# A post-norm decoder layer: the context projected in tiles of 125 tokens instead of batch by batch

## The reference

```python
x = layernorm(x + self_attention(x))            # 16 heads of 16, rotary
x = layernorm(x + cross_attention(x, ctx))      # 16 heads of 64
x = layernorm(x + mixture_of_experts(x))        # 14 experts, top 1

# cross attention
Q = einsum('bsd,hdk->bhsk', queries, WQ) + bQ
K = einsum('btd,hdk->bhtk', keys, WK) + bK
V = einsum('btd,hdv->bhtv', values, WV) + bV    # keys and values are both the context
scores = Q @ K / 8
allowed = (key <= query) & (key < length[b])
concat = softmax(where(allowed, scores, -1e6)) @ V
out = concat @ WO + bO
```

## Time and profile before

| | |
|---|---|
| runs shown | 529.42, 529.50, 530.25 us, median 529.5 |
| profiled execution | 529.48 us |
| its span, first to last instruction | 527.7 us |
| mean granted TensorE clock | 0.96 |
| busy PE / DVE / ACT / POOL | 89% / 67% / 58% / 40% |

### The profile page before, as it was taken

One profiled execution on the slowest core, in us unless ns is written; L12 is line 12 of the kernel. 1 busy time (PEld: TensorE's weight loads), 2 busy tenths in 40 slices (PEclk: granted clock), 3 DMA queues, 4 the chain that ended last, 5 costly groups with the idle time before them and its releaser, 6 DMA issues. The chain is left out here.

```text
span 527.7 us, 12522 instructions
## 1 busy us (share of the span) xinstructions
PE 471.4 (89%) x4430; PEld 402.1 (76%) x4430; DVE 353.8 (67%) x971; ACT 304.2 (58%) x1400; POOL 211.1 (40%) x293
## 2 busy tenths in 40 slices
PE   1688899999998999999999999999999763999991
PEld 0566688878797888778887988788798662999981
DVE  1699686867869875887669658963745544255553
ACT  2266575888575674677576667783846612333330
POOL 1457543454246544443343433731413302144443
PEclk9899799999999999999999999999999985899997
DMA  5971444402600406304314104100405523999100
GB/s 167 203 163 43 166 169 166 162 2 101 220 8 22 162 17 232 114 0 160 135 34 144 45 1 153 47 1 2 161 1 181 186 115 100 368 371 372 44 25 17
DMA packets 38200, 63.03 MB, mean 119 GB/s; under 512 B 10435, under 2 KB 31412, under 8 KB 37419
## 3 DMA queue, kind: packets, MB, share of 16 engines
q1 hardware_dynamic: 34742, 33.03, 20.5%
q10 hardware_dynamic: 926, 25.83, 13.9%
q0 software_dynamic: 2464, 3.31, 2.0%
HBM read 58.85 MB, written 29.77 MB: 168 GB/s over the span
## 5 line engine op out<-in xcount | busy, mean ns | idle before, releaser
L972 ACT ACTIVATE probs<-bank,neg_max 100x100 f32<-100x100 f32 x512 | 169.8, 369 | 28.9 <-DVE neg_max L1096 18.0
L886 POOL TENSOR_TENSOR probs<-probs,row_inv 100x400 f32<-100x400 f32 x128 | 109.6, 877 | 110.4 <-DVE row_inv L1101 110.2
L972 ACT ACTIVATION_READ_ACCUMULATOR probs<-bank,neg_max 100x1 f32 x512 | 117.8, 230 | 0.0
L1096 DVE TENSOR_REDUCE neg_max<-bank 100x4 f32<-100x400 f32 x128 | 67.9, 565 | 9.9 <-PE bank L1367 4.8
L1401 PE MATMUL bank<-ident,probs 100*100 100x100 f32 x512 | 67.8, 255 | 5.7 <-DVE probsT L1108 4.1
L1401 PEld LDWEIGHTS bank<-ident,probs 100*100 100x100 f32 x512 | 50.4, 130 | 18.6 <-issue 7.5
L981 ACT COPY probsT<-bank 100x400 f32<-100x400 f32 x60 | 29.8, 497 | 47.2 <-PE bank L1401 41.5
L1245 PE MATMUL bank<-cT_h,W_K 128*128 128x200 f32 x256 | 50.6, 284 | 0.7 <-DVE kX L1024 0.6
L1318 PE MATMUL bank<-yT,W_Q 128*128 128x250 f32 (+1 forms) x224 | 50.3, 367 | 0.0
L1108 DVE COPY probsT<-bank 100x400 f32<-100x400 f32 x68 | 38.7, 569 | 16.3 <-PE bank L1401 14.4
L1245 PEld LDWEIGHTS bank<-cT_h,W_K 128*128 128x128 f32 x256 | 41.6, 193 | 2.5 <-DVE kX L1024 1.3
(11 more groups left out here) (153 smaller groups left out, 972.6 us busy)
## 6 DMA issues: line engine op xcount, KB each, us to landing
expert_rows<-c_empty ACTq DMA_DIRECT2D x13, 1935.0 KB, 8.9
w<-in_L_ffn_w_dram SPq DMA_DIRECT2D x36, 512.0 KB, 6.8
cs<-in_ctx_dram SPq DMA_DIRECT2D x16, 100.0 KB
...
```

Source lines behind the costliest of these rows:

```text
L886: probs_ready.mark(pool.tensor_tensor(v, v, r, ALU.mult), step)
L972: i = act.activation(probs[:, k % SLOTS, w], sc_bank[p % 2 * 2 + u][0:T, w], ACT.Exp, bias=neg_max[:, k % SLOTS, h:h + 1], accum_out=row_s ...
L1096: max_ready.mark(dve.tensor_reduce(neg_max[:, k % SLOTS, :], src, AX_X, ALU.max, negate=True), step)
```

## The change

- The context is loaded, turned and split in the 13 tiles of 125 tokens. A tile's rows come from two batches, so `c_load.n` is now up to two DMAs into one slot of `cs`, each with its own look at the length. `cT` holds 250 tokens.
- Keys are projected for two tiles, 250 columns at a time (7 groups instead of 8; the last has 100 columns). `kX` is a ring of 500 tokens.
- Values are projected per tile: `V.t.c` (13 tiles instead of 16 batches) goes to a staging buffer `v_tile` with one slot for each half, through a plain copy by DVE or ACT (`V_out_v`, `V_out_a`). A new step `move.b.c.t`, a DMA on SP's queue, copies the rows of tile t that belong to batch b from `v_tile` to `vX`. There are 50 of them, of 25 to 100 rows of 2 KB. `pv.x.b.c` waits for their landing, `V_out` of tile t+1 waits for the landing of tile t's moves, and a move waits for `V_out` and for `pv.x.(b-2).c`.
- The bias of the values goes through WO once: `vb_hi` (ACT) and `vb_lo` (DVE) spread and split it, `vb.0` (PE, 24 matmuls of 256 columns) multiplies it by WO, and `vb_out` (DVE) adds it to `o_bias`. `v_bias` is loaded as 128 x 8 by eight small DMAs that stand at the end of SP's first DMAs; the broadcast of 100 x 1024 is gone.
- `Y2S` goes from 6 to 4, `cs` slots are 125 rows, the buffer `fix` shares space with `oX`. `check` of batch 2 moves ahead of the list.
- `STEPS` is a new list throughout.

```diff
-Y2S = 6
+Y2S = 4
...
-check.2 check.3 xT.0 check.4 xT_hi.0 bias.s.0 xT_lo.0 check.5 w_hi.0 xT.1 check.6 w_hi.1 w_lo_v.0 bias.s.1 xT_hi.1
...
+check.3 xT.0 check.4 xT_hi.0 bias.s.0 xT_lo.0 check.5 w_hi.0 xT.1 check.6 w_hi.1 w_lo_v.0 bias.s.1 xT_hi.1 w_lo_v.1
...
+check.13 check.14 qkT.0 qk_out.1 qkT_out_a.0 check.15 xT.3 rot.1 xT_hi.3 keys_p.0 cT.1 w_hi.5 c_load.3 xT_lo.3
+bias.s.3 scores.s.0.0 rot_sum.1 cT_hi.1 w_lo_p.5 cT_lo.1 cT.2 max.s.0.0.0 qkT.1 c_load.4 max.s.0.0.1 exp.s.0.0.0
...
+def shared_rows(b, t):
+    first, last = max(T * b, TT * t), min(T * (b + 1), TT * t + size(t))
+    return slice(first - T * b, last - T * b), slice(first - TT * t, last - TT * t)
...
-            v_bias = ab("v_bias", [T, DC])
+            v_bias = ab("v_bias", [P, PAIRS])
...
-            cT = [ab(f"cT_{p}", [P, CTS, KC, KB * T], F32R) for p in "hl"]
+            cT = [ab(f"cT_{p}", [P, KC, QT], F32R) for p in "hl"]
...
-            kX = ab("kX", [P, 2, PAIRS, KB * T])
+            kX = ab("kX", [P, PAIRS, RT])
             vX = ab("vX", [T, 2, DC])
+            v_tile = ab("v_tile", [TT, 2, DC // 2])
...
+            def values_there(b, c, t=None):
+                k = 2 * (b % 2) + c
+                parts = sum(len(tiles_of(n)) for n in range(b % 2, b, 2)) + (len(tiles_of(b)) if t is None else t - tiles_of(b)[0] + 1)
+                return v_moved[k], 16 * parts
...
+                elif kind == "V":
+                    if step[1]:
+                        for b in batches_of(step[1] - 1):
+                            wait(*values_there(b, n, step[1] - 1))
...
                 def load_c(n):
-                    wait(ctx_fixed, n + 1)
                     if n >= 2:
                         wait(*projected.at(("cT", n - 2)))
-                    length = sp.value_load(len_row[0:1, n:n + 1])
...
+                    for b in batches_of(n):
+                        wait(ctx_fixed, b + 1)
+                        of_batch, of_tile = shared_rows(b, n)
+                        length = sp.value_load(len_row[0:1, b:b + 1])
...
+                            sp.dma_start(cs[of_tile, n % 2, :], ctx[b, of_batch, :]).then_inc(c_in[n % 2], 16)
+
+                def move(b, c, t):
+                    wait(*taken(("V", t, c)))
+                    if b >= 2:
+                        wait(*pv_done.at(("pv", "x", b - 2, c)))
+                    of_batch, of_tile = shared_rows(b, t)
+                    sp.dma_start(vX[of_batch, b % 2, c * (DC // 2):(c + 1) * (DC // 2)], v_tile[of_tile, c, :]).then_inc(v_moved[2 * (b % 2) + c], 16)
...
-                    (v_bias[:, :], bV.rearrange("(o h) k -> o (h k)", o=1).broadcast_to([T, DC])),
...
+                bias_by_head = bV.rearrange("(c w i u) d -> c i u d w", c=2, w=2, i=2, u=2)
+                for c, i, u in np.ndindex(2, 2, 2):
+                    sp.dma_start(v_bias[i * DK:(i + 1) * DK, c * UH + 2 * u:c * UH + 2 * u + 2], bias_by_head[c, i, u],
+                                 allow_slow_non_contiguous=True).then_inc(route_in, 16)
...
-                for last, first in ((("out", NT - 1), 0), (("K", B // KB - 1, PAIRS // KM - 1), 2), (("V", B - 1, 1), 4)):
+                for last, first in ((("out", NT - 1), 0), (("K", NQ - 1, PAIRS // KM - 1), 2), (("V", NT - 1, 1), 4)):
...
-                        if t == "cT" and g >= CTS:
-                            wait(*projected.at(("K", g - CTS, PAIRS // KM - 1)))
-                            wait(*projected.at(("V", KB * (g - CTS + 1) - 1, 1)))
+                        if t == "cT" and n >= 2:
+                            wait(*projected.at(("K", n // 2 - 1, PAIRS // KM - 1)))
+                            wait(*projected.at(("V", n - 2, 1)))
...
+                    elif kind == "vb":
+                        wait(*taken_by["vector"].at(("vb_lo", 0)))
+                        i = three(ps[0:TT, 0:D], [[t[:, m, 0:TT] for m in range(PAIRS)] for t in oX], [[t[:, m, :] for m in range(PAIRS)] for t in WOs])
+                        projected.mark(i, step)
```

More of the change, by code:

```diff
@@ L92 @@
[L92 to L101, removed]
@@ new lines @@
+cT_lo.2 out.0 move.0.1.0 move.1.1.0 v.3 added.s.0 stats.s.0 turn.s.2.1.0 scores.s.3.0 copy_a.s.2.1.0 v_out.3
+rstd.s.0 turn.s.2.1.1 max.s.3.0.0 V.1.0 copy_a.s.2.1.1 max.s.3.0.1 exp.s.3.0.0 max.s.3.1.0 ln.s.0 pv.s.2.1
+V_out_v.1.0 exp.s.3.0.1 x_load.4 yT.0 max.s.3.1.1 move.1.0.1 v.4 bias.x.0 yT_out_v.0 o_hi.s.2.1 V.1.1 inv.s.3.0
+exp.s.3.1.0 v_out.4 norm.s.3.0.0 o_lo.s.2.1 norm.s.3.0.1 out.1 exp.s.3.1.1 V_out_v.1.1 turn.s.3.0.0 move.1.1.1
+added.s.1 xT.4 copy_v.s.3.0.0 cT.3 xT_hi.4 bias.s.4 scores.s.4.0 c_load.5 stats.s.1 cT_hi.3 turn.s.3.0.1 max.s.4.0.0
@@ new lines @@
+copy_a.x.3.0.0 o_lo.s.7.1 norm.x.3.1.1 turn.x.3.0.1 v_out.9 qkT.7 copy_a.x.3.0.1 rstd.x.1 cT.5 qkT_out_a.7
+scores.x.4.0 c_load.7 ln.x.1 cT_hi.5 keys_p.8 keys_v.9 turn.x.3.1.0 cT_lo.5 max.x.4.0.0 out.5 copy_a.x.3.1.0
+max.x.4.0.1 exp.x.4.0.0 rT.1 added.s.5 scores.x.4.1 rT_out_v.1 stats.s.5 exp.x.4.0.1 logits.1 max.x.4.1.0 K.2.0
+rstd.s.5 logits_out.1 exp.x.4.1.0 mask.5 ln.s.5 turn.x.3.1.1 K_out_v.2.0 K.2.1 x_load.9 copy_a.x.3.1.1 inv.x.4.0
+max.x.4.1.1 norm.x.4.0.0 top.0 exp.x.4.1.1 yT.5 K_out_v.2.1 pv.x.3.0 norm.x.4.0.1 choose.0 count.0 K.2.2 bias.x.5
@@ new lines @@
+move.5.1.4 move.6.1.4 v.10 rT_out_v.3 turn.x.5.0.0 o_hi.s.8.1 v_out.10 logits.3 exp.s.9.1.0 inv.s.9.0 o_lo.s.8.1
+Q.2.2 norm.s.9.0.0 copy_v.x.5.0.0 logits_out.3 norm.s.9.0.1 top.1 gate.1 choose.1 count.1 out.6 Q_out_a.2.2
+turn.x.5.0.1 added.s.6 copy_a.x.5.0.1 rank.1 stats.s.6 exp.s.9.1.1 Q.2.3 place.1 rstd.s.6 ln.s.6 turn.s.9.0.0
+scatter.2 Q_out_a.2.3 cT.6 copy_v.s.9.0.0 scores.s.10.0 x_load.10 c_load.8 cT_hi.6 inv.s.9.1 turn.s.9.0.1 cT_lo.6
+scatter.3 max.s.10.0.0 yT.6 copy_a.s.9.0.1 V.5.0 max.s.10.0.1 yT_out_a.6 max.s.10.1.0 exp.s.10.0.0 bias.x.6
@@ new lines @@
+v_out.14 qkT.11 copy_a.x.8.0.1 rstd.x.5 cT.9 qkT_out_a.11 scores.x.9.0 c_load.11 ln.x.5 cT_hi.9 keys_p.13 keys_v.14
+turn.x.8.1.0 cT_lo.9 max.x.9.0.0 out.9 copy_a.x.8.1.0 max.x.9.0.1 exp.x.9.0.0 rT.5 added.s.9 scores.x.9.1 rT_out_v.5
+stats.s.9 exp.x.9.0.1 logits.5 max.x.9.1.0 K.4.0 rstd.s.9 logits_out.5 exp.x.9.1.0 mask.10 ln.s.9 turn.x.8.1.1
+K_out_v.4.0 K.4.1 copy_a.x.8.1.1 inv.x.9.0 max.x.9.1.1 norm.x.9.0.0 top.2 exp.x.9.1.1 yT.9 K_out_v.4.1 pv.x.8.0
+norm.x.9.0.1 choose.2 count.2 K.4.2 bias.x.9 yT_out_a.9 o_hi.x.8.0 gate.2 o_lo.x.8.0 rank.2 inv.x.9.1 K_out_a.4.2
@@ new lines @@
+move.10.1.8 move.11.1.8 v.15 rT_out_v.7 turn.x.10.0.0 o_hi.s.13.1 v_out.15 logits.7 exp.s.14.1.0 inv.s.14.0
+o_lo.s.13.1 Q.4.2 norm.s.14.0.0 copy_v.x.10.0.0 logits_out.7 norm.s.14.0.1 top.3 gate.3 choose.3 count.3 out.10
+Q_out_a.4.2 turn.x.10.0.1 added.s.10 copy_a.x.10.0.1 rank.3 stats.s.10 exp.s.14.1.1 Q.4.3 place.3 rstd.s.10 ln.s.10
+turn.s.14.0.0 scatter.6 Q_out_a.4.3 cT.10 copy_v.s.14.0.0 scores.s.15.0 c_load.12 cT_hi.10 inv.s.14.1 turn.s.14.0.1
+cT_lo.10 scatter.7 max.s.15.0.0 yT.10 copy_a.s.14.0.1 V.9.0 max.s.15.0.1 yT_out_a.10 max.s.15.1.0 exp.s.15.0.0
@@ L793, in do @@
                         load_c(n)
+                    elif kind == "move":
+                        move(*step[1:])
                 for step in PLAN:
@@ L1262, in do @@
                         wait(ident_in, 16)
[L1263 removed]
+                        w = size(n)
                         if kind == "xT":
```

394 lines of the change are left out of this document (198 added, 196 removed).

## The result

The changed kernel takes 539.24 us (median of 4 runs, 537.26 to 539.74) against 529.88 us (529.42 to 531.3, 4 runs) on the same chip: ratio 1.0167, 95% interval 1.0146 to 1.0187. The profiled execution took 539.74 us, its span 538.0 us. Forecast were 540 us in a range of 529 to 553.

What follows compares the result with a forecast made beforehand. PE's work was taken to bound the middle, data arrival and hand-overs the start. 527.7 + 19.8 (later `out.0`) - 11.0 (matmuls) + 1.5 (moves) = 538.0 us span, plus 1.8 around it: about 540 us, range 529 to 553.

Steps and rivals of the forecast that it cites:

- What bounds the kernel: Whole kernel: PE's own work bounds 66 to 420 us (busy 345 of 354); data arrival and engine hand-over bound the start.
- Two of its signs: Before `out.0`: PE busy under 12 us in the first 48; waits for bank 6's takers of 5 us or more.
- PE's work from the paces: PE's matmuls: V 8.3, K 4.6 and cT 0.6 us less, vb 2.9 more; net 10.6 us less.
- the one by columns: K projections: if cost follows columns, K saves nothing and PE's net saving is 6.0 us.
- the sum of -11.0 behind `out.0`: From `out.0` on: the whole 10.6 us of PE savings and 0.4 more come off here.
- the +1.5 for the moves: The 50 move DMAs: a few have tight readers; cost 1.5 us, bounds -1 and +9.
- The third cT: Start, at `cT.2`: PE stands until the late third tile lands at 48.2 us, bounds 46.3 and 52.
- From there to `out.0`: Stretch from `qkT.1` to `out.0`: 33 us, bounds 26 and 38; `out.0` at 81.6, 19.8 us later.
- 13 turnovers of 0.9 us: Before `out.0`: 13 projections in a row share bank 6, each waiting about 0.9 us until the one before is taken.
- The count of matmuls decides: Whole kernel: without the early stall, or with slack to absorb it, 519 us, or up to 528; chance 0.10.
- It cancels: Whole kernel: `out.0` at 70 to 73 us, so 528.4 to 530.5 us; chance 0.04.
- The moves collide with the clearings: Moves issued during ACT's 13 clearings: half a dozen delayed 3.5 us each, 10 to 15 us extra, 550 to 555; chance 0.14.

Runs made afterwards that it cites:

- the kernel with the early load: Changed kernel with the third context tile's load issued right behind the load of the lengths on SP, list unchanged: 521.15 us, ratio 0.9843.
- the fastest one: Changed kernel with `cT.2` moved to right ahead of `cT_hi.2` and `c_load.4` to behind `move.1.1.1`: 518.02 us, ratio 0.9784.
- the run without them: Changed kernel without the eight small `v_bias` DMAs and the steps `vb_hi`, `vb_lo`, `vb`, `vb_out`: 533.51 us, ratio 1.0061.
- the one that stands at the old place: Changed kernel with `cT.2` and `c_load.4` right ahead of `cT_hi.2`, PE only waiting for the third tile where `cT.2` was: 543.84 us, ratio 1.0264.

## Why the prediction was right

**What bounds the kernel.** It said that a gain has to come from the middle and a loss from the start. Both did: -9.2 and +19.8 us. Two of its signs did not come: PE is busy for 12.84 us up to its restart, not under 12, and from there to `out.0` it waits 3.5 us for the takers of bank 6 (4.4 us idle in all), not 5 or more.

**PE's work from the paces.** The K step shown above takes 239.42 - 237.92 = 1.50 us; over the 22 such steps at the full clock the median is 1.495, where 1.46 was taken and a step of 200 columns has 1.42. The four steps of 100 columns take 1.27 to 1.36. So K costs about 0.4 us more than forecast, and of the two ends the one by columns (1.42 x 250/200 = 1.78) is out. The rule of the Trainium skill (TensorE: Matmul & The Clock Gate, LDWEIGHTS and Back-to-back issue gap) was read as 250 columns costing no more than 200; the steps show 5% more, and by the rule the sum would have been further off. That page of the Trainium skill gives N/2.4 + 2.5 as the gap of an isolated matmul and not of a stream, which the prediction left out; these steps are a stream. V's steps of 125 rows take 1.49 us as the median of 26, against 1.45 for 100 rows in the kernel before (the 1.38 of the earlier trace rows was the shortest of them), so V saves 46.4 - 38.7 = 7.7 us and not 8.3. Both savings were put a little too high, and yet the sum of -11.0 behind `out.0` is what the kernel with the early load shows (365.5 against 376.5 us), and the fastest one exceeds it (60.73 to 425.41 is 364.7). PE's waits in the middle fell as well: by the list of its waits they are 8.4 us from `out.0` to 420 us in the kernel before and 5.9 in the changed one. The changed kernel has only -9.2, with the same moves as the two others. So the +1.5 for the moves, which made the forecast's -9.5 look exact, had the wrong name: PE waits 0.4 us in all for `v_tile`, and the 1.8 us are lost only behind the long stand. Between `out.0` and the last `rank` PE is idle for 15.2 us in the changed kernel and 15.7 with the early load, but busy for 352.1 against 349.8 with the same 3585 matmuls. So the 1.8 us are no wait but slower matmuls. The changed kernel has 3.4 us more at half clock from 95.8 to 99.2, and 3.4 more within 426.9 to 433.8; that these make the whole 1.8 us is argued, not shown.

**The third cT.** 48.2 us forecast, 46.63 measured, 18.67 us of wait. Eight v_bias DMAs at 4.2 were 5.15 us; the 1 us for two more loads ahead did not appear, and SP's first DMAs ran about 1.7 us earlier than before. That the queue's time becomes PE's one to one is shown by the run without them: 5.1 us.

**From there to `out.0`.** 33 us forecast, 34.5 measured, so that `out.0` came at 81.55 against 81.6: two errors of 1.5 us that cancel, which is luck. Of its parts, the old pace was put at 32.3 us, and with the bank free it is 30.6; the single bank is shown at 3 to 4 us, where 13 turnovers of 0.9 us were counted and all but 0.7 us of them taken as filled; the half clock behind the stand, some 0.9 us, was put at nothing past the first transposes. The 2.9 us of `vb`, counted in full, cost next to nothing there, and this is the step that was wrong in kind: in a stretch with 4.4 us of idle PE, and DVE as the one it waits for, PE's matmuls are no sum.

**The rivals.** The count of matmuls decides: it does as soon as the stand is gone, at 521 and 518 us, against the 519 that this rival gave. It cancels: no. The moves collide with the clearings: not in the changed kernel, whose PE waits for no DMA but the first loads and the third tile until the experts. But in others DVE waits 7 to 9 us for one move, and the price, put at 10 to 15 us for half a dozen moves at 3.5 us each, comes from a single clash at 8 to 9 us. The 3.5 us of the earlier trace rows were too small a bound for it. By the Trainium skill (DMA: Bandwidth & Descriptors, Queues, rings and completion order) a DMA engine goes round the queues packet by packet, and I drew from it that a move loses at most a packet or two of a clearing, without asking how long such a packet is. The trace of the kernel before shows it, in 4 us of a clearing (286 to 290 us: packets, MB, share of 16 engines):

```profile
q10 hardware_dynamic: 36, 1.59, 116.5%
```

A packet is 44 KB and takes 1.165 x 16 x 4 / 36 = 2.1 us. A clearing is 45 of them, about three on each engine: an estimated 6 us. A DMA whose small packets take turns with these can lose all three. The runs show 10.4 us against 4.25, so the load lost about that, and the conclusion of "a packet or two and not a whole clearing" doesn't hold; the rule itself is not contradicted. That the turns are taken so is argued from these sizes, not shown. A chance of 0.14 for it was not too high: the changed kernel misses the clash by 0.9 us.

**What stays open.** Whether any clearing would do it or only this one, and when a move is held: three kernels have DVE wait 7 to 9 us for a move whose issue runs into this clearing's, and the one that stands at the old place has 0.9 us for such a move. The clearing is issued 7.9 us after the first, within the 8.9 us that the page of the profile gives as the median of one. Within 1 us behind the other clearings no run issues a load, only moves (at the eighth and the thirteenth), and PE doesn't wait for those; the two that were issued in a row at 85 us caught nothing, but nothing that PE needed soon was issued behind them.
